# Two layers of attention and experts: where a carried chunk of work stands inside an attention turn, and in which turns the expert weights are prepared

## The reference, cut to what matters

```python
x = tokens                                                   # 4 sequences of 512 tokens, 128 wide
x = x + 0.5 * ffn0(layernorm(x))                             # ternary weights, 128 -> 512 -> 128, relu
x = x + attn0(layernorm(x))                                  # 16 heads of 64, causal, sigmoid gates
x = x + 0.5 * ffn0(layernorm(x))
x = x + 0.5 * moe1(layernorm(x))                             # 8 experts, top 2, silu(xW1) * xW3, W2
x = x + attn1(layernorm(x))                                  # 16 heads of 64, causal
x = x + 0.5 * moe1(layernorm(x))
```

## Time and profile before

| | us |
|---|---|
| median of 3 runs (981.19 to 983.82) | 981.59 |
| profiled execution, its own time | 980.19 |
| its span on the core | 978.4 |
| PE busy | 847.4 (87%) |
| DVE busy | 787.3 (80%) |
| POOL busy | 741.2 (76%) |
| ACT busy | 642.5 (66%) |
| mean granted TensorE clock | 0.965 |

### The profile page before, as it was taken

One profiled execution on the slowest core, in us unless ns is written; L12 is line 12 of the kernel. 1 busy time (PEld: TensorE's weight loads), 2 busy tenths in 40 slices (PEclk: granted clock), 3 DMA queues, 4 the chain that ended last, 5 costly groups with the idle time before them and its releaser, 6 DMA issues.

```text
span 978.4 us, 32967 instructions
## 1 busy us (share of the span) xinstructions
PE 847.4 (87%) x12648; PEld 598.8 (61%) x12648; DVE 787.3 (80%) x2498; ACT 642.5 (66%) x1119; POOL 741.2 (76%) x685
## 2 busy tenths in 40 slices
PE   5788989888888776999996889999999985899994
PEld 3446666566656555776773556666766765576673
DVE  6878989879788876897776779798989987696773
ACT  6767878677766553766774657666676764466662
POOL 6769999979987773677663699797888885677772
PEclk9999999999999997999997999999999999899997
DMA  5122432432135231122312022232222322212232
GB/s 156 51 60 45 83 88 40 89 82 56 40 45 120 50 41 36 59 50 50 92 42 63 19 45 41 47 58 46 56 51 51 52 56 40 60 47 51 95 69 85
DMA packets 123516, 58.92 MB, mean 60 GB/s; under 512 B 106978, under 2 KB 112866, under 8 KB 123364
## 3 DMA queue, kind: packets, MB, share of 16 engines
q1 hardware_dynamic: 116128, 43.68, 21.2%
q0 software_dynamic: 5888, 12.07, 4.9%
q10 hardware_dynamic: 1348, 1.05, 0.3%
HBM read 22.44 MB, written 9.18 MB: 32 GB/s over the span
## 4 chain that ended last, share of the span: by engine, by line
PE 57%; DVE 22%; POOL 9%; issue 6%; ACT 5%; DMA 2%; SPq 0%; POOLq 0%; DVEq 0%; ACTq 0%
PE ps L1910 8%; PE ps L1731 7%; DVE ps L1339 7%; PE ps L1732 6%; PE ps L1733 6%; POOL arena L829 5%; PE ps L2138 4%; PE ps L1884 3%; PE ps L1943 2%; PE ps L2151 2%; PE ps L2150 2%; PE ps L2152 2%; PE ps L1944 2%; PE ps L1945 2%; DVE arena L1339 1%
## 5 line engine op out<-in xcount | busy, mean ns | idle before, releaser
L829 POOL TENSOR_TENSOR arena<-arena 128x1024 f16<-128x1024 f32 x190 | 346.0, 1822 | 89.7 <-ACT arena L1025 79.6
L1017 ACT ACTIVATE arena<-ps,lift 128x1024 f32<-128x1024 f32 (+1 forms) x192 | 187.9, 979 | 161.3 <-PE ps L1920 152.7
L1339 DVE CUSTOM_DVE_ANT_0 ps<-ps,mask_qk 128x512 f32<-128x512 f32 (+3 forms) x512 | 238.9, 519 | 28.0 <-PE ps L1884 27.1
L1943 PE MATMUL ps<-arena 128*128 128x65 f16 x1280 | 127.8, 195 | 45.5 <-DVE arena L1230 14.2
L1910 PE MATMUL ps<-arena 64*128 64x512 f16 (+3 forms) x1536 | 149.6, 300 | 11.4 <-ACT arena L1017 11.2
L1943 PEld LDWEIGHTS ps<-arena 128*128 128x128 f16 x1280 | 115.9, 97 | 61.9 <-DVE arena L1230 15.5
L880 POOL DMA_INDIRECT arena<-x_rows,arena x92 | 90.9, 989 | 57.5 <-PE ps L2113 22.1
L1944 PE MATMUL ps<-arena 128*128 128x64 f16 x1280 | 127.0, 193 | 0.0
L1945 PE MATMUL ps<-arena 128*128 128x65 f16 x1280 | 126.6, 193 | 0.0
L888 POOL DMA_INDIRECT y_rows<-arena x92 | 91.0, 989 | 43.5 <-issue 22.8
L1945 PEld LDWEIGHTS ps<-arena 128*128 128x128 f16 x1280 | 117.5, 98 | 0.0
(11 more groups left out here) (283 smaller groups left out, 2612.3 us busy)
## 6 DMA issues: line engine op xcount, KB each, us to landing
stage<-in_L_ffn_W SPq DMA_DIRECT2D x4, 1024.0 KB, 6.0
arena<-y_rows SPq DMA_DIRECT2D x14, 256.0 KB, 3.8
x_rows<-XN SPq DMA_DIRECT2D x8, 256.0 KB, 2.3
arena<-x_rows,arena POOLq DMA_INDIRECT x92, 2.7
y_rows<-arena POOLq DMA_INDIRECT x92, 2.3
stage<-in_L_attn_Wkv SPq DMA_DIRECT2D x2, 512.0 KB, 8.1
arena<-arena SPq DMA_TRANSPOSE x64, 2.3
T<-arena SPq DMA_TRANSPOSE x64, 3.4
```

The lines of the kernel that those rows point to most:

```text
L829: g.tensor_tensor(PL[:, b, :, cols], P32[:, :, cols], PH[:, b, :, cols], ALU.subtract).then_inc(s_pl, 1)
L1017: a_.activation(P32[:, :, UNIT_AT[u]:UNIT_AT[u] + UNIT_W[u]], ps[:, 4:6, 0:UNIT_W[u]], ACT.Exp, bias=lift[:]).then_inc(s_ex_p, 1)
L1339: v_.tensor_tensor_reduce(ps[:, 2 + x, at:at + w], ps[:, 2 + x, at:at + w], mask_qk[:, CH - w:CH], 1.0, NEG, ALU.add, ALU.max, accum_out=M ...
L1943: mm(ps[:, bank, c:c + DH + 1], ph_, VH[:, r, k, x, 0:DH + 1], start=(k == 0), stop=False)
```

## The change

Four edits in one.

1. PE: `filled()` goes ahead of `project_v`. ACT: the carried chunk's operation goes ahead of `p_high` and `v_high`. DVE: it goes ahead of maxima of unit 1, and `route` is cut in two: `route_logits`, which frees the bank, ahead of these maxima, and `route_top` behind them.
2. Maxima of unit 2: in turns 0 to 2 PE and DVE no longer make them at the end of the turn, but in the next turn behind the projections (PE) and `k_low` (DVE).
3. The quarter blocks go to turns 2 to 31 without 6, 8, 14, 20, 22 and 28. The turns of `expert_block` follow: 6, 12, 17, 22 in place of 6, 10, 14, 18.
4. `second_layer` goes from turn 27 to turn 32.

```diff
+        QUARTER_TURNS = tuple(t for t in range(2, 32) if t not in (6, 8, 14, 20, 22, 28))
         def quarters(t):
-            return (t - 2,) if 2 <= t < 26 else ()
+            return (QUARTER_TURNS.index(t),) if t in QUARTER_TURNS else ()
...
-                    if a == 0 and t in (6, 10, 14, 18):
-                        expert_block((t - 6) // 4 + 2)
-                    if a == 0 and t == 27:
+                    if a == 0 and t - 1 in QUARTER_TURNS[3:16:4]:
+                        expert_block(quarters(t - 1)[0] // 4 + 2)
+                    if a == 0 and t == 32:
                         second_layer()
...
# ACT
                         exps(1)
+                    if kind == "turn":
+                        turned_x(n, c)
+                    if kind == "up":
+                        hidden_high(1, n, c)
+                    if kind == "gate":
+                        gate_exp(c)
+                    if s is not None:
                         if last:
                             p_high_last(1)
                         else:
                             p_high()
                     if p is not None:
                         v_high()
-                    if kind == "turn":
-                        turned_x(n, c)
-                    if kind == "up":
-                        hidden_high(1, n, c)
-                    if kind == "gate":
-                        gate_exp(c)
...
# DVE
                         q_low()
                         k_low()
+                        if 0 < t <= LAGS[3]:
+                            maxima(2, m - 1)
                     if m is not None and maxima_too:
-                        maxima(0)
+                        maxima(0, m)
...
-                    if m is not None and maxima_too:
-                        maxima(1)
                     if kind == "turn":
                         turned_x(n, c)
...
                     if kind == "route":
-                        route(n, c)
+                        route_logits(n, c)
+                    if m is not None and maxima_too:
+                        maxima(1, m)
+                    if kind == "route":
+                        route_top(n, c)
...
-                    if m is not None and maxima_too:
-                        maxima(2)
+                    if m is not None and t >= LAGS[3]:
+                        maxima(2, m)
...
# PE
                         project_q()
                         project_k()
+                        if 0 < t <= LAGS[3]:
+                            maxima(2, m - 1)
...
                         project_out()
+                    filled()
                     if p is not None and projections_too:
                         project_v()
-                    filled()
...
-                    if m is not None and maxima_too:
-                        maxima(2)
+                    if m is not None and t >= LAGS[3]:
+                        maxima(2, m)
```

More of the change, by code:

```diff
@@ L488, in k_bank @@
             return 7
+        QUARTER_TURNS = tuple(t for t in range(2, 32) if t not in (6, 8, 14, 20, 22, 28))
+        assert len(QUARTER_TURNS) == 4 * len(experts)
         def quarters(t):
-            return (t - 2,) if 2 <= t < 26 else ()
+            return (QUARTER_TURNS.index(t),) if t in QUARTER_TURNS else ()
         def hidden(f, c, k):
@@ L1248, in gate_one, with route_logits @@
                 v_.tensor_scalar(gs, gs, 1.0, None, ALU.add).then_inc(s_g_one, 1)
-            def route(m, c):
+            def route_logits(m, c):
                 dve.wait_ge(s_r_ps, NCH * m + c + 1)
@@ L1256, in route, with route_top @@
                                  ).then_inc(s_r_lg, 1)
+            def route_top(m, c):
+                lg = logits[:, TPC * c:TPC * (c + 1), :]
                 dve.wait_ge(s_r_lg, NCH * m + c + 1)
@@ L1327, in body, with maxima @@
                     p, m, s, v, o, z = items(t)
-                    def maxima(u):
+                    def maxima(u, m):
                         j = base + m
@@ L1650, in carried @@
                     if t == 7:
-                        route(0, 2)
+                        route_logits(0, 2)
+                        route_top(0, 2)
                     if t == 9:
@@ L1654, in carried @@
                     if t == 10:
-                        route(0, 3)
+                        route_logits(0, 3)
+                        route_top(0, 3)
                     routed(0, t - 11)
@@ L1672, in carried @@
                     if t == 3:
-                        route(1, 3)
+                        route_logits(1, 3)
+                        route_top(1, 3)
                     routed(1, t - 4)
```

## The result

| kernel | median, us | runs, us | ratio, 95% interval |
|---|---|---|---|
| before | 981.59 | 981.01 to 984.59 | |
| after | 949.77 | 947.01 to 951.23 | 0.9662, 0.9638 to 0.9686 |

A forecast was written before the change was run, and what follows sets the result against it. PE was taken to set the pace, waiting for DVE's part of the carried chunk. Attention 0 -17.3 and attention 1 -11.9 make -29.2 us from 980.19, so 951.0, written 951.5; likeliest case 942 to 959, range 941 to 966.

The forecast's parts named there:

- the likeliest case: Whole kernel: the forecast case, 942 to 959 us around 951.5, chance 0.62.
- "up" turns: Turns 15 to 18 and 23 to 26 of attention 0, 10.01 us each before; eight together forecast to gain 6.9 us.
- PE waits for DVE's part of the chunk, and this goes: At PE's first `outputs(1)` matmul: 40.6 us in 30 waits, 1.27 us idle per "up" turn, which would go.
- The forecast bound of 8: Sign to check: PE's wait at `outputs(1)` for four named DVE lines and logits under 8 us, in place of 40.6.
- The ring through `p_high`: POOL in "up" turns: exp of unit 1, `p_high`, two low parts, cast; 7.5 becomes 8.6 us, under PE's 8.73.
- The price of `output_low`, 9.15 a turn: DVE in "up" turns: `output_low` stands behind POOL's L728, costing 0 to 1.16 us; 9.15 a turn, bounds 8.73 and 10.01.
- Turns 2 to 14, 19 to 22, 27 to 31: Attention 0 stretches: -3.3 us with the start's +0.65 included, -2.1 and -5.5.
- The expensive neighbour, ACT: ACT between exp of unit 1 and `p_high`: a late carried chunk there delays `p_high`; 993 us, chance 0.05.
- The slower case: Rival: `k_low` behind POOL delays chunk and `p_high`, ring 10.7 us against 10.01; 993 us, chance 0.05.
- Maxima of unit 2 deferred: Turns 0 to 2: six PE waits of 1.74 us go; +0.65 us in attention 0, -2.0 in attention 1.
- The start of attention 0: Before turn 2: PE's `maxima(0)` waits for `k_low` and moved maxima, a gate chunk precedes `p_high`; +0.65 us.
- The fills of attention 1: Turns 8 to 10 -2.8 us, 14 to 16 and 22 to 24 -2.35 each, 30 to 32 -1.9, 2 to 7 -0.5; sum -9.9.

## Why the prediction was right, point by point

The time forecast was 951.5 and came out 949.8, inside the likeliest case, and the profiled spans agree with the sum within 0.2. That closeness owes much to luck. The profiled execution before (980.19) is under the lowest of its five runs, the one after (951.23) is the highest of its five, and the medians differ by 31.8, 2.6 more than the sum. Inside the sum the "up" turns and turns 27 to 31 gained 3.0 more than forecast, turns 2 to 7 of attention 1 lost 3.2 against it.

*PE waits for DVE's part of the chunk, and this goes.* Right. 40.6 became 5.5 for all waits at that line, and DVE's order put back alone brings the 1.27 us of each "up" turn back. The forecast bound of 8 held.

*The ring through `p_high` just fits.* Right where it is full: POOL is busy 8.58 of 8.74 us. PE's order put back, which delays `p_high` by 0.67, makes the turn 0.42 longer: the ring had 0.25 us to spare.

*The price of `output_low`, 9.15 a turn.* The mechanism was right and the size was one bound and the other. In turns 15 to 18 it took 0.87 to 1.03 us, hidden, and the turns are PE's 8.74; it met unit 2's low part there, and not L731. DVE did not become the busiest engine, as the forecast had it: it is busy 8.34 of 8.74. In 23 to 26 it took 1.37 to 1.55 us and the turns 9.0 to 9.2, as this row of turn 24 and POOL's beside it show:

```profile
256.96 1.15 POOL L731 TENSOR_TENSOR E2l<-stage,E2h 128x512 f16<-128x512 f32 x1
257.11 1.55 DVE L1371 TENSOR_TENSOR arena<-arena 128x512 f16<-128x512 f32 x1
```

`output_low` began 0.15 us after `quarter_low` and ended 0.55 us after it: it took 0.86 more than its 0.69, most of the 1.00 that L731 still had to run. So it stood behind L731, as the Trainium skill, "SBUF — State Buffer", section "SBUF: two separate sides", would have it. The mean of the eight turns is 8.91. With the maxima not deferred all eight are 8.73 to 8.82: there `output_low` begins 0.65 us or more into unit 2's low part in each: the price hangs on tenths of a us. So the mistake of 1.9 us here is to have given all turns the same overlap. All 64 together went from 50.4 to 57.2 us.

*Turns 2 to 14, 19 to 22, 27 to 31.* Right within 1.1 each. In 27 to 31 DVE's 45.96 is what I had worked out (45.8), POOL's 44.48 too (44.4), and no blocked `output_low` of 2.5 us is left.

*The expensive neighbour, ACT.* The slower case (`k_low` blocked, so the chunk late, so `p_high` late) did not occur: no "up" turn is above 9.2.

*Maxima of unit 2 deferred.* This step failed, though the total hides it. The start of turn 2 of attention 1 came earlier by about what I said (the way there 2.1 shorter against 1.5), but I priced only the semaphores that PE waits for and left SP out: the row maxima leave DVE one projection later, and with them the DMA transpose that the scores wait for. Turns 2 and 3 took 19.8 in place of 15.7. With the maxima in their own turn they take 17.1. The 1.4 between 15.7 and 17.1 goes with the granted clock in turn 2, 0.96 before against 0.81 there, and the kernel with the quarters and `second_layer` alone, where attention 1 is untouched, has it too (17.1, with 0.80). So the deferral costs these two turns between 2.7 and 4.1, by the kernel that it is held against. That is not all waiting. Turn 2 holds the 1.86 us for the transpose; turn 3, behind it, is 2.3 longer than in the kernels without deferral, at a granted clock of 0.83, with PE busy 9.31 where it had been 7.47:

```profile
517.76:527.47 9.71, 5.82 (x81) 3.44 (x82) 6.37 (x22) 5.62 (x7) 4.14 (x3) 1.00 0.23 15
527.47:537.53 10.06, 9.31 (x143) 5.69 (x142) 6.54 (x23) 5.44 (x8) 7.71 (x7) 0.83 0.07 15
```

Turns 4 to 7 then took 37.2 in place of 38.6. In all the gain of this edit, forecast at 2.0 in attention 1, is zero within the 0.3% (950.17 and 949.77).

*The start of attention 0.* The table's +0.6 for a forecast +0.65 is chance. Kernels with the same order up to that point put the first exponential of turn 2 at 54.20 and 55.18, or at 54.58 and 55.98. The four with the whole deferral have it at 52.4 to 54.1 and the seven without at 53.5 to 56.0, so no cost at the start is seen. What the forecast left out is behind it: turns 2 and 3 of attention 0 take 19.0 to 19.8 with the deferral and 16.7 to 18.2 without.

*The fills of attention 1.* Turns 14 to 16, 22 to 24 and 30 to 32 right within 0.4. Turns 8 to 10 gave 1.5, not 2.8: DVE is busy 25.38 and POOL 25.50 of 28.50. I take it that I had not allowed for their shares lying unevenly over the three turns; no run shows that. The 28.50 comes again without the deferral and without the quarters, so it belongs to the chunk's own step. The 29.98 before is the looser number: with the chunk in its old place and the same order in attention 1 it was also 31.54. Turns 11 to 13, priced at 0, gave 0.7.

Turns 29 and 31 take 12.2 us with the chunk alone; in the changed kernel and the two that differ from it in the deferral alone, turn 31 takes 10.4 and turn 29 10.9 to 12.9. In turn 31 most of the difference goes with the granted clock, as its windows show with the chunk alone and with the maxima not deferred:

```profile
326.03:338.24 12.21, 10.12 (x156) 6.89 (x156) 10.21 (x40) 6.55 (x9) 7.47 (x6) 0.86 0.15 34
```
```profile
317.46:327.84 10.38, 8.77 (x156) 6.15 (x156) 9.90 (x33) 7.50 (x11) 9.23 (x7) 1.00 0.35 30
```

PE is busy 1.35 us longer with the same 156 matmuls. Ahead of `project_q` it had stood 1.43 us in the first and 0.95 in the second. Why that idle is shorter with the quarters spread stays open: no run took it apart.

## What to carry to other kernels

When one piece of work goes through three engines in turn, move it on all three and price each order by itself: here with DVE's order left behind 28.6 of the 31.8 us are lost, with ACT's 21.8 (3.6 of them by two blocked operations elsewhere), with PE's 8.0. Relieving an engine (POOL, 0.2% alone) pays only after the wait that sets the pace is gone, and then it paid 9 us. When a step is delayed, follow its result to the DMA that carries it: maxima read later cost 1.86 us of idle through a transpose on SP's queue, and more behind it at a lower granted clock. And compare stretches only with the granted clock beside them: the same order of work took 1 to 1.5 us more in a turn where it was lower.

## What the runs showed of the hardware

When a two-operand SBUF operation of DVE meets one of POOL that began before it, the operation of DVE gets longer, and so does the next one of POOL if it follows at once; the one that it met does not. `output_low`, begun 0.17 us into POOL's low part, took 2.50 us. The low part kept its 2.13, and POOL's cast behind it then took 1.50 in place of 1.03, as it met the rest of `output_low`. In the "up" turn, `output_low` took 0.95, begun 0.76 us into a low part of 1.16, and `quarter_low` behind that 1.61 in place of 1.16. So the total delay is larger than the one instruction that the waits name.

A gap on PE can also cost behind its end. Turns 2 and 3 of attention 1, with 4.6 us of idle on PE, ran at a mean granted clock of 0.91, while turns 15 to 18 show 1.00. The 2 us from 527.47 on have 0.53, nearly all of it the lower of the two levels (1.2 GHz). Behind the 1.86 us of idle at 526.37 a matmul of 128x512 took 0.63 us, where it is 0.38 in the "up" turn (L1765 at 192.90):

```profile
527.96 0.63 PE L1748 MATMUL ps<-XTh,WQl 128*128 128x512 f16 x1
```
```profile
192.90 0.38 PE L1765 MATMUL ps<-XTl,F 128*128 128x512 f16 x1
```

It does not follow each time: behind the same 1.6 us of idle in turn 29 of attention 0 the turn had 1.00 in one kernel and 0.87 in the other (above). No run shows what decided it. In turns 27 to 31 the mean went from 0.97 to 1.00. That is a gain that no term of the sum had by itself.
